# Four transformer layers in one kernel: scores earlier in the MLP part, key and value projections together between the tiled runs

## The reference

```python
for layer in range(4):
    sh1, sc1, g1, sh2, sc2, g2 = modulation(layer, cond)        # the last layer has no g1, g2
    h = norm(x) * (1 + sc1) + sh1
    q, k, v = split(h @ Wqkv)                                    # 16 heads of 16
    s = q @ k.T / 4                                              # layer 1: causal; layer 3: q and k rotated (rope)
    x = x + g1 * (softmax(s) @ v) @ Wo
    h = norm(x) * (1 + sc2) + sh2
    x = x + g2 * act(h @ W1 + b1) @ W2                           # gelu; layer 3: a * silu(gate), W1 twice as wide
```

## Time and profile before

| | us |
|---|---|
| median of 3 runs | 2266.0 (2265.19 to 2268.1) |
| the profiled execution, whole | 2262.32 |
| its span, first to last instruction | 2260.4 |
| a step with tiles of layer 0 | 31.52 |
| a step with tiles of layer 1 | 32.05 |
| a step with tiles of layer 2 | 31.66 |
| a step with tiles of layer 3 | 38.58 |

### The profile page before, as it was taken

The page is one execution under the profiler, slowest core; times in us unless marked ns, Lnnn a source line. Parts: engine busy times, 40 slices in busy tenths (PEclk is TensorE's granted clock), DMA queues, the critical chain, the costliest instruction groups (busy, mean ns, idle before and its releaser), DMA issues.

```text
span 2260.4 us, 63283 instructions
## 1 busy us (share of the span) xinstructions
PE 2155.1 (95%) x20080; PEld 1807.2 (80%) x20080; DVE 1697.4 (75%) x4339; ACT 1249.8 (55%) x2618; POOL 1086.4 (48%) x1333
## 2 busy tenths in 40 slices
PE   4699999999999999999999999999999999999997
PEld 2488888888888888888878888888778888787877
DVE  2677777777776777677778777777788888888873
ACT  1366666666565555555676666666654454435441
POOL 2244455455544454445454554446454545444434
PEclk7799999999999999999999999999999999999998
DMA  5422112222222112212331122222222121111210
GB/s 194 131 72 73 63 63 68 70 71 77 85 91 71 62 60 70 74 61 81 102 99 64 60 69 75 66 63 74 86 72 73 55 67 58 63 60 61 65 58 15
DMA packets 164671, 166.11 MB, mean 73 GB/s; under 512 B 29296, under 2 KB 143856, under 8 KB 164560
## 3 DMA queue, kind: packets, MB, share of 16 engines
q1 hardware_dynamic: 164560, 164.69, 22.7%
HBM read 58.47 MB, written 4.39 MB: 28 GB/s over the span
## 4 chain that ended last, share of the span: by engine, by line
PE 84%; DVE 6%; issue 3%; SPq 2%; ACT 1%; POOL 1%; DMA 1%; POOLq 0%; ACTq 0%; DVEq 0%
PE B L530 36%; PE B L630 14%; PE B L799 10%; PE B L776 7%; PE B L577 7%; PE B L639 4%; PE B L649 2%; PE B L733 2%; DVE NEGM L1018 2%; SPq L1407 2%; PE B L554 2%; DVE G L1025 1%; ACT PR L944 1%; ACT G L912 0%; POOL GHl L1300 0%
## 5 line engine op out<-in xcount | busy, mean ns | idle before, releaser
L944 ACT ACTIVATE PR<-B 128x512 f32<-128x512 f32 (+1 forms) x1024 | 504.9, 570 | 282.8 <-PE B L776 280.1
L1300 POOL TENSOR_TENSOR GHl<-G,GHh 128x256 fp32r<-128x256 f32 x512 | 377.6, 738 | 475.2 <-ACT GHh L918 288.4
L1018 DVE TENSOR_REDUCE NEGM<-B 128x2 f32<-128x512 f32 x768 | 485.0, 683 | 91.9 <-PE B L577 91.9
L530 PE MATMUL B<-H2h,W1h 128*128 128x256 f32 x1280 | 397.8, 311 | 3.1 <-issue 3.1
L530 PE MATMUL B<-H2h,W1l 128*128 128x256 f32 x1280 | 363.2, 284 | 0.0
L530 PE MATMUL B<-H2l,W1h 128*128 128x256 f32 x1280 | 362.7, 283 | 0.0
L918 ACT ACTIVATE G<-B,VEC 128x256 f32<-128x256 f32 x384 | 182.0, 474 | 284.2 <-PE B L530 284.2
L630 PE MATMUL B<-W2h,GHh 128*128 128x256 f32 x1024 | 297.1, 290 | 1.7 <-POOL GHl L1300 1.7
L630 PE MATMUL B<-W2l,GHh 128*128 128x256 f32 x1024 | 290.3, 283 | 0.0
L630 PE MATMUL B<-W2h,GHl 128*128 128x256 f32 x1024 | 289.6, 283 | 0.0
L530 PEld LDWEIGHTS B<-H2h,W1h 128*128 128x128 f32 x1280 | 244.3, 191 | 44.4 <-issue 26.4
(11 more groups left out here) (160 smaller groups left out, 4704.1 us busy)
## 6 DMA issues: line engine op xcount, KB each, us to landing
QS<-QHL SPq DMA_DIRECT2D x768, 64.0 KB, 2.1
KS<-KHL SPq DMA_DIRECT2D x768, 64.0 KB, 2.1
GA<-gate_scratch SPq DMA_DIRECT2D x48, 256.0 KB, 3.2
GM<-gate_scratch SPq DMA_DIRECT2D x48, 256.0 KB, 3.4
RAW<-in_w SPq DMA_DIRECT2D x36, 256.0 KB, 3.5
CW<-in_cw SPq DMA_DIRECT2D x3, 1536.0 KB, 12.4
QS<-MT SPq DMA_DIRECT2D x256, 4.0 KB
GA<-in_rows_last SPq DMA_DIRECT2D x16, 256.0 KB, 3.3
```

The source lines that it names most:

```text
L530: last = nc.tensor.matmul(dst, w[i], x[j], start=(first_k and n == 0), stop=(last_k and n == 2))
L944: nc.scalar.activation(PR[:, h % PRING].rearrange("p k q -> p (k q)")[:, 0:n], src[:, 0:n], ACT.Exp, scale=SCALE).then_inc(ac_exp, 1)
L1018: last = nc.vector.tensor_reduce(NEGM[:, :, c], src, op=ALU.max, axis=AX.X, negate=True)
L1300: nc.gpsimd.tensor_tensor(GH[1][:, j % RING, :], G[:, j % RING, :], GH[0][:, j % RING, :].bitcast(F32), ALU.subtract).then_inc(po_gl, 1)
```

## The change

- **MLP part.** `up(3)`, `down(1)` go behind S01, `down(2)` behind S23, `up(6)` behind S45. The last scores (S67) stand where they stood, between `down(5)` and the rest, and `down(6)` now follows them with `down(7)`.
- **Behind the MLP.** T01 and the turned maxima come directly behind `down(7)`; the query projection follows. T23 and PV0 come next as one run, then key and values (24 matmuls) in one group, with `norm_2` behind them (for tiles of the last layer it stands before T23), then T45, PV1, T67, PV2, PV3.
- **Banks.** T01 to T67 use four banks, 2, 3, 1 and 4, instead of six; the last score goes to bank 6, query and values to 5, key to 0, `norm_2` to 7.
- **Layer 3.** DVE adds the PSUM result to `X` itself (`add_to_x`), with the bias rows added by POOL earlier; `statistics_2` stands at j = 5 instead of behind the MLP.
- **Maxima rows.** One DMA for eight heads instead of two. On ACT the second `MT` copy stands behind the second exp, not the first. On DVE the maxima and the normalisation of tile t+1 move one place forward.

```diff
-S_BANKS = (4, 5, 0, 1) * 3 + (4, 5, 0, 2)
+S_BANKS = (4, 5, 0, 1) * 3 + (4, 5, 0, 6)
...
-ST_BANKS = ((4, 5, 0, 7) * 2 + (4, 5, 1, 3) * 2, (4, 5, 0, 7) * 2 + (4, 5, 0, 1) * 2)
-NORM2_BANK = (0, 7)
+ST_BANKS = (2, 3, 1, 4) * 4
+Q_BANK, K_BANK, V_BANK = 5, 0, 5
+NORM2_BANK = 7
...
                 up_if(2)
                 down_if(0)
-                up_if(3)
-                down_if(1)
                 if s.r is not None:
                     outputs_to_features()
                 scores_if(0)
                 scores_if(1)
+                up_if(3)
+                down_if(1)
                 up_if(4)
-                down_if(2)
                 if s.r is not None:
                     output_projection()
                 scores_if(2)
                 scores_if(3)
+                down_if(2)
                 up_if(5)
                 down_if(3)
                 if s.q is not None:
                     norm_1()
-                up_if(6)
-                down_if(4)
                 scores_if(4)
                 scores_if(5)
+                up_if(6)
                 if scored:
                     maxima_to_rows(0)
+                down_if(4)
                 up_if(7)
-                down_if(5, 6)
+                down_if(5)
                 scores_if(6)
                 scores_if(7)
-                down_if(7)
-                query(0)
-                query(1)
+                down_if(6, 7)
                 if scored:
                     transposed_pairs(0, 1)
                     maxima_to_rows(1)
+                query(0)
+                query(1)
+                if s.r is not None and (s.lr == ROPE or not scored):
+                    norm_2()
+                if scored:
+                    transposed_pairs(2, 3)
+                    outputs(0)
                 key(0)
                 key(1)
                 if scored:
-                    transposed_pairs(2, 3)
                     values(0)
-                    outputs(0)
+                    values(1)
+                    if s.r is not None and s.lr != ROPE:
+                        norm_2()
                     transposed_pairs(4, 5)
                     outputs(1)
-                    if s.r is not None:
-                        norm_2()
                     transposed_pairs(6, 7)
                     outputs(2)
-                    values(1)
                     outputs(3)
...
-                        if h == 0:
+                        if h == 1:
                             rows_of_maxima(1)
...
+            def add_to_x(sequence, s_bias, n, src):
+                x = X[:, seq(sequence), :, :].rearrange("p a t d -> p (a t) d")
+                dv.wait_ge(s_bias, n + 1)
+                apart(dv)
+                return nc.vector.tensor_tensor(x, x, src, ALU.add)
...
-                    for half in range(2):
-                        row = ROWS * half + STK
-                        sp.dma_start(QS[row:row + 1, HQ * part:HQ * part + HQ, :].bitcast(F32),
-                                     MT[HQ * half:HQ * half + HQ, part, :].bitcast(F32)).then_inc(sp_mt[part], 16)
+                    slots = slice(HQ * part, HQ * part + HQ)
+                    sp.dma_start(QS[STK:STK + ROWS + 1:ROWS, slots, :].bitcast(F32),
+                                 MT[:, part, :].bitcast(F32)).then_inc(sp_mt[part], 16)
```

More of the change, by code:

```diff
@@ L568, in score_pair @@
                         at_least(pe, dv_on, 2 * s.r_done)
[L569 to L572 removed]
+                    elif before[1] is None and banks[2 * p + 1] == 6:
+                        pe.wait_ge(ac_mt, 2 * a_ + 1)
                     for i in range(NT):
@@ L701, in key @@
                         return
-                    if f == 0:
-                        hidden_read(s)
-                        key_read(s)
-                    last = project(bank(3)[:, f, :], cols(wq, D + f * P), H1)
+                    if f == 0 and scored:
+                        pe.wait_ge(dv_max, H * s.a + last_user(S_BANKS + (K_BANK,), H) + 1)
+                    last = project(bank(K_BANK)[:, f, :], cols(wq, D + f * P), H1)
                     if f == KD - 1:
@@ L712, in values @@
                         return
-                    if scored and i == 0:
-                        pe.wait_ge(dv_max, H * (s.a + 1))
+                    if i == 0 and rope:
+                        pe.wait_ge(dv_rot, 2 * (s.q - NSEQ * ROPE) + 1)
                     elif i == 0:
-                        hidden_read(s)
-                        at_least(pe, dv_v, s.nq)
+                        pe.wait_ge(dv_q, s.q + 1)
                     for k in range(KD):
-                        last = product(bank(2)[:, i, :], [x[:, k, i * P:(i + 1) * P] for x in H1],
+                        last = product(bank(V_BANK)[:, i, :], [x[:, k, i * P:(i + 1) * P] for x in H1],
                                        [w[:, k, 2 * D:3 * D] for w in wq], k == 0, k == KD - 1)
@@ L791, in outputs @@
                         at_least(pe, dv_dn, s.m_done)
-                        if rope and s.r is not None:
+                        if s.r is not None:
                             pe.wait_ge(dv_f2, s.r + 1)
@@ L922, in body @@
                         new_weights(FIRST)
-                    if j == 3 and s.r is not None:
+                    if j == 2 and s.r is not None:
                         outputs_hi(s)
@@ L1079, in normalise_1, with statistics_2 @@
                     normalise(XQ, tokens(sequence), MV1, RS1, dv_xn1, layer == ROPE)
+                def statistics_2():
+                    if s.r is not None:
+                        if s.lr == ROPE:
+                            dv.wait_ge(dv_wo, s.r + 1)
+                            apart(dv)
+                        else:
+                            dv.wait_ge(po_x1, s.r + 1)
+                        statistics(tokens(s.sr), ST2, MV2, dv_st2, dv_mv2, s.r)
                 for j in range(NJ):
@@ L1107, in body @@
                         maxima(3)
+                        if s.lr == ROPE:
+                            statistics_2()
+                        maxima(4)
                     if j == 6:
                         split_1()
[L1110 to L1111 removed]
                         maxima(5)
                 maxima(6)
+                maxima(7)
                 if s.m is not None:
                     dv.wait_ge(pe_dn, NJ * s.m + NJ)
[L1117 to L1125 removed]
+                    if s.lm == ROPE:
+                        add_to_x(s.sm, po_xb2, s.m, bank(7)).then_inc(dv_dn, 1)
+                    else:
+                        if s.lr != ROPE:
+                            at_least(dv, po_x1, s.r_done)
+                        multiply(bank(7), GM, sp_gm, s.m).then_inc(dv_dn, 1)
                 def normalise_2():
@@ L1303, in body @@
                         rstd(MV1, RS1, TV1, dv_mv1, po_t1, po_rs1, s.q, s.lq)
-                    if j == 4 and s.r is not None:
+                    if j == (1 if s.lr == ROPE else 4) and s.r is not None:
                         residual_1_bias(s)
-                    if j == 5 and s.r is not None:
+                    if j == 3 and s.lm == ROPE:
+                        residual_2_bias(s)
+                    if j == 5 and s.r is not None and s.lr != ROPE:
                         residual_1(s)
@@ L1309, in body @@
                         low_1(s)
-                if s.m is not None:
+                if s.r is not None and s.lr == ROPE:
+                    rstd(MV2, RS2, TV2, dv_mv2, po_t2, po_rs2, s.r, s.lr)
+                if s.m is not None and s.lm != ROPE:
                     m, xm = s.m, x_of(s.sm)
-                    po.wait_ge(dv_xn2, m + 1)
-                    po.wait_ge(sp_gm, 16 * (m + 1))
-                    apart(po)
-                    nc.gpsimd.tensor_tensor(xm, xm, GM[:, 1:2, :].to_broadcast([P, NT, D]), ALU.add).then_inc(po_xb2, 1)
+                    residual_2_bias(s)
                     po.wait_ge(po_xb2, m + 1)
@@ L1359, in store @@
             def store(s, tile, sequence):
-                hold(po_x2, tile + 1)
+                hold(dv_dn, tile + 1)
                 o = out[seq(sequence), :, :].rearrange("a (t p) d -> p (a t) d", p=P)
```

123 lines of the change are left out of this document (59 added, 64 removed).

## The result

| | us |
|---|---|
| before, median of 4 runs | 2265.6 (2262.43 to 2268.1) |
| changed, median of 4 runs | 2333.53 (2331.74 to 2334.43) |
| ratio | 1.0300, 95% interval 1.0282 to 1.0317 |
| the profiled execution of the changed kernel, whole | 2334.43 |
| its span | 2332.3 |

The change makes the kernel 68 slower; 2336 was forecast, and 2333.5 lies in the range. All times are in microseconds. An even step is one in the middle of a layer; such steps repeat to a few hundredths.

A forecast was written before the change was run, and what follows sets the result against it. PE, busy 95% of the span, was taken as the bound; 27.8 + 17.3 - 12.0 + 27.2 + 6.4 + 2.9 = 69.6 on the profiled 2262.3 gave 2332, plus 3.7 for the median: 2336 us, range 2298 to 2354.

The forecast's parts named there:

- T45 to PV3 (ACT sets the end): Stretch behind the MLP, layers 0 and 2: the last eight exps set its end, 5.87, with 1.6 of waiting.
- Layers 0 and 2, the other pieces: down(5) up to T45, priced piece by piece; with T45's 5.87 the stretch is 17.06 against 16.19, +27.8 over 32 tiles.
- The MLP part: 46 other scored steps: turned maxima cost 0.22 instead of 0.13, S45 brushes DVE for 0.05; +6.4 in all.
- Layer 1: Behind T45 5.72 against 5.74, but norm_2 and six products now stand ahead: 1.08 a tile, +17.3 over 16 tiles.
- Layer 3 behind the MLP: A gain of 0.75 a tile over 16 tiles, -12.0, with S67 no longer waiting for a bank.
- S67's wait goes: Layer 3: S67's second pair no longer waits for free bank 2, -0.60.
- Layer 3, MLP part: 14 scored steps: S45 waits 1.25 for DVE's maxima, S01 0.6 for KS; 1.94 a step, +27.2.
- The clock is no term: Whole kernel: every step runs at granted clock 1.00, the 2.4 GHz level, so the clock was given no cost.
- Only the switches: Rival, T45 to PV3: exps keep pace with PE, three switches fewer save 0.42 in 62 steps; 2240, chance 0.10.
- Layer 3's waits covered: Rival: neither of the two new waits in layer 3's MLP part shows; 2310, chance 0.16.
- Turned maxima as a tiled group: Rival: between full products the turned maxima cost two further switches of 0.2 in 62 steps; 2361, chance 0.06.
- Nothing: Rival, whole kernel: gain and waits cancel, the time staying within 0.2% of 2266; chance 0.03.

The follow-up runs named there:

- half_after: Changed kernel with exps of 256 columns instead of 512 (384 in layer 1), second half of the probabilities left out: 2266.7 us, ratio to before 1.0027.
- half_before: Kernel before the change with exps of 256 columns, second half of the probabilities left out: 2236.2 us, ratio to before 0.9887.
- maxima_first: Changed kernel, but DVE takes the maxima of heads 6 and 7 ahead of the gate product of up(5): 2304.7 us, ratio to before 1.0194.
- combo_a: Changed kernel; norm_2, values behind PV1/PV2 again (layers 0-2), maxima 6, 7 before gate product, weight splits behind maxima, layer 3 DMAs by group: 2249.3 us, ratio 0.9948.
- swap_half: Changed kernel with exps of half size, and in layer 3 POOL takes H2's low half ahead of the sum for key: 2289.0 us, ratio to before 1.0123.

## Why the prediction was right

The time was right to 3, and the mechanism that carried it is shown. That the time came so close is luck: the terms of even steps were too high, and the steps in which a layer begins or ends cost twice what it had for them.

- **T45 to PV3 (ACT sets the end).** Right. 5.69 instead of 5.87: the eight exps in a row take 4.03, which is a pace of (4.03 - 0.60)/7 = 0.49 and not 0.507, and 7 x 0.017 makes 0.12 of the 0.18. half_after and half_before show that the exps were the whole loss in even steps of layers 0 and 2. In layer 3 the number came out (5.94), but the mechanism was another: POOL's low half of H2.
- **Layers 0 and 2, the other pieces.** down(5) to T01 3.18 (3.09), T01 with turned maxima 0.90 (0.93), query 1.62 (1.61), T23 0.96 (1.05), key and values 2.95 (2.98), norm_2 0.53. The tail takes 16.83 where 17.06 was forecast, +0.64 instead of +0.87. The MLP part adds 0.07 instead of 0.14.
- **Layer 1.** +0.85 instead of 1.22. T45 to the end is 5.69 (5.72). Before, the masks of T01 and of T23 had waited some 0.1 each, and I had not seen that these waits would go; and the MLP part costs nothing here.
- **Layer 3 behind the MLP.** -0.63 instead of -0.75; S67's wait goes, as said.
- **Layer 3, MLP part.** S45 waits 1.28 (forecast 1.25), S01 0.46 (0.6). maxima_first and combo_a show both causes. An even step comes to 39.75 (39.8).
- **The sum.** For the 47 even steps these terms make 51.8 (25 x 1.01 + 12 x 1.22 + 10 x 1.19), and 37.9 were measured. For the 16 others they leave 17.8, and 36.6 were measured. The two errors, -13.9 and +18.8, nearly cancel, and the 3 that come back outside the 63 steps take off half of the rest.
- **The step that failed.** "The clock is no term": it is none in even steps, but in six steps at the layers' starts the clock falls behind the new waits, which costs about 12 in all. I had read the clock in two even steps of before, said it of every step, though steps 48 and 49 of before are at 0.95 and 0.96, and carried it over to after. And DVE's weight splits were in no term. They stand at the same j in both kernels, but the calls around them have moved, and S45 now follows norm_1 directly, so it waits for the maxima behind them. I had priced only the calls that run in every step.
- **Rivals.** Only the switches: fell. The pieces behind the MLP do show them: with short exps T01 to `up(0)` is 0.24 shorter than before (query counted in both), less than 0.42. Layer 3's waits covered: fell, both are there. Turned maxima as a tiled group: fell. The next product starts 0.14 behind the first of the two, and its group of six takes 0.79 where 0.72 is dense, so they cost 0.2 in all as forecast, and no two further switches. Nothing: fell, the time is 3% up.

## What to carry to other kernels

An engine that is idle for long ahead of a serial run of another engine's work is the place where gathered work goes missing: before products are put together in a dense group, ask which wait they were filling, and whether the group can stand so that the wait still has something in it. Price the steps where a loop's pattern breaks (here the 16 at the layers' starts) apart from the even ones. Where several chains end within a microsecond of each other, shortening one gives nothing until the next is shortened too. And two short waits can be cheaper than one long one (1.3 and 0.5 against 1.75 in swap_half, by 1.5 a step), but three short ones close together brought the clock down as well (step 17).
